# Local products of the first three sequences split between VectorE and GpSimd, late weights held back

## The reference

```python
x = x + local_attention(layernorm(x))            # each token sees itself and 3 tokens on each side
x = x + cross_attention(layernorm(x), ctx_1024)  # 120 context tokens
z = layernorm(x)                                 # then a block with its own residuals:
z = z + causal_attention(rmsnorm(z, n1_w))
z = z + silu(rmsnorm(z, n2_w) @ up.T) @ down.T * gate_factor
x = x + z
```

## Time and profile before

| | |
|---|---|
| median of 3 runs | 3523.06 us (3519.29 to 3523.43) |
| profiled execution: its time | 3525.48 us |
| its span | 3523.7 us |
| mean granted clock of TensorE | 0.986 |
| busy: TensorE / VectorE / ScalarE / GpSimd | 3421.1 / 2680.4 / 1829.9 / 2499.1 us |
| products of the local attention on GpSimd | 880.0 us (v) and 552.2 us (k) |
| their sums on VectorE | 294.4 us (v) and 291.7 us (k) |

### The profile page before, as it was taken

The page is one execution under the profiler, slowest core; times in us unless marked ns, Lnnn a source line. Parts: engine busy times, 40 slices in busy tenths (PEclk is TensorE's granted clock), DMA queues, the critical chain, the costliest instruction groups (busy, mean ns, idle before and its releaser), DMA issues.

```text
span 3523.7 us, 91852 instructions
## 1 busy us (share of the span) xinstructions
PE 3421.1 (97%) x36229; PEld 2775.1 (79%) x36229; DVE 2680.4 (76%) x5867; ACT 1829.9 (52%) x4241; POOL 2499.1 (71%) x3160
## 2 busy tenths in 40 slices
PE   5699999999999999999999999999999999999997
PEld 4477888888888888888888888888888888888876
DVE  5687787787787787787787787787787787787763
ACT  2345545545545545545545545545545545545542
POOL 5677777777777777777777777777777777777731
PEclk8799999999999999999999999999999999999998
DMA  5111221121121221121121221221121121121200
GB/s 169 61 52 47 69 77 47 69 77 47 69 77 47 69 77 47 69 77 47 69 77 47 69 77 46 69 77 47 69 77 47 69 77 47 69 77 47 69 8 10
DMA packets 90149, 223.31 MB, mean 63 GB/s; under 512 B 9286, under 2 KB 56706, under 8 KB 73346
## 3 DMA queue, kind: packets, MB, share of 16 engines
q1 hardware_dynamic: 89730, 217.44, 18.0%
HBM read 164.92 MB, written 50.39 MB: 61 GB/s over the span
## 4 chain that ended last, share of the span: by engine, by line
PE 95%; DVE 2%; ACT 1%; POOL 1%; DMA 0%; issue 0%; SPq 0%; DVEq 0%; ACTq 0%
PE ps L892 13%; PE ps L901 13%; PE ps L763 11%; PE ps L870 10%; PE ps L819 10%; PE ps L741 9%; PE ps L797 9%; PE ps L842 8%; PE ps L769 4%; PE ps L721 3%; PE ps L791 1%; PE ps L808 1%; PE ps L856 1%; ACT prob L1006 1%; DVE nmax L1328 1%; DMA y<-in_ctx 0%
## 5 line engine op out<-in xcount | busy, mean ns | idle before, releaser
L1162 POOL TENSOR_TENSOR chunks<-v_windows,xT 128x560 f32<-128x560 f32 (+1 forms) x384 | 880.0, 2302 | 85.5 <-DVE xT L1303 76.6
L1328 DVE TENSOR_REDUCE nmax<-ps 128x4 f32<-128x480 f32 (+2 forms) x1280 | 776.8, 671 | 178.0 <-PE ps L797 178.0
L1006 ACT ACTIVATE prob<-ps 128x256 f32<-128x256 f32 (+2 forms) x1536 | 670.5, 557 | 436.0 <-PE ps L819 436.0
L1157 POOL TENSOR_TENSOR chunks<-rest,k_windows 128x512 f32<-128x512 f32 (+1 forms) x384 | 552.2, 1454 | 366.7 <-DMA k_windows<-passed_on 291.7
L1282 DVE TENSOR_REDUCE held<-chunks 128x80 f32<-128x560 f32 (+1 forms) x384 | 294.4, 767 | 303.3 <-POOL chunks L1162 297.0
L892 PE MATMUL ps<-xT,w_up 128*128 128x256 f32 x2048 | 485.2, 385 | 1.6 <-ACT xT L959 1.6
L901 PE MATMUL ps<-w_down,held 128*128 128x256 f32 x2048 | 459.0, 382 | 1.9 <-DVE held L1381 1.6
L901 PEld LDWEIGHTS ps<-w_down,held 128*128 128x128 f32 x2048 | 383.9, 190 | 59.7 <-DVE held L1381 1.9
L892 PEld LDWEIGHTS ps<-xT,w_up 128*128 128x128 f32 x2048 | 375.2, 191 | 70.5 <-issue 20.2
L959 ACT COPY xT<-ps 128x512 f32<-128x512 f32 x256 | 153.1, 598 | 355.1 <-PE ps L721 355.1
L1174 POOL TENSOR_SCALAR_AFFINE_SELECT prob<-prob 128x512 f32<-128x512 f32 x512 | 310.9, 641 | 35.9 <-ACT prob L1006 35.8
(11 more groups left out here) (150 smaller groups left out, 6719.6 us busy)
## 6 DMA issues: line engine op xcount, KB each, us to landing
k_windows<-passed_on SPq DMA_DIRECT2D x64, 1024.0 KB, 5.0
v_windows<-passed_on SPq DMA_DIRECT2D x64, 1024.0 KB, 5.0
x<-in_x SPq DMA_DIRECT2D x64, 256.0 KB, 2.9
passed_on<-rest SPq DMA_DIRECT2D x64, 256.0 KB, 2.0
passed_on<-held SPq DMA_DIRECT2D x64, 256.0 KB, 3.4
out<-x SPq DMA_DIRECT2D x64, 256.0 KB, 2.2
y<-in_ctx SPq DMA_DIRECT2D x64, 120.0 KB, 2.8
held<-nmaxT SPq DMA_DIRECT2D x256, 8.0 KB
```

The costliest lines, as they stand in the source:

```text
L1006: last = nc.scalar.activation(prob_pair(seq, L, m)[0:keys, :, r, col:col + qs], of_pair, ACT.Exp, scale=SCALE)
L1157: last = nc.gpsimd.tensor_tensor(chunk_of(c).rearrange("p (j d) -> p j d", d=D), q_row, window("k", (b + first) * D, (D, n), (1, D)), ALU. ...
L1162: last = nc.gpsimd.tensor_tensor(chunk_of(c).rearrange("p (h i j) -> p h i j", i=HD, j=WINDOW), window("v", b * D + first * HD, (HD, n), ( ...
L1328: nc.vector.tensor_reduce(of_heads[:, ms[0]:ms[-1] + 1, :, r], src, AX_X, ALU.max, negate=True).then_inc(emptied[b], 1)
```

## The change

**What it does.** (a) For the first three sequences (EARLY = 3) the products of the even chunks 0, 2, 4, 6, 8, 10 move to VectorE; GpSimd keeps the odd ones. A helper, times, issues the same tensor_tensor on either engine. VectorE's products signal a new semaphore, doubled. The window buffers' next fetch waits for both engines, and GpSimd's chunks 1 and 7 wait for the windows and the softmax themselves, as chunks 0 and 6 did. From s3 on all twelve are GpSimd's. (b) BEHIND holds back two groups of weights in SyncE's list: group 3 is offered when the fetch of s0's k window has been issued, group 4 after that of its v window. (c) The constants that GpSimd writes at the start become a part of the plan, in the same place of its list. (d) Planner figures: transfers get a size and share an assumed wire, TensorE's parts take longer after an idle time, and busy times, lags and the cost of changing tiling are altered. These have no effect but on the lists.

Cut to the core; what is left out is the longer form of part(), further altered busy times of the same kind, and the constants' code, which moves as it is.

```diff
-Part = namedtuple("Part", "name args engine busy lag after takes gives")
-LAG = {"PE": 0.21, "ACT": 0.15, "DVE": 0.15, "POOL": 0.1}
+Part = namedtuple("Part", "name args engine busy lag after takes gives kb", defaults=(0,))
+LAG = {"SP": 1.1, "PE": 0.21, "ACT": 0.2, "DVE": 0.2, "POOL": 0.1}
 DMA_ISSUE = 0.42
 PLACES = {"lane": LANES, "prob": PROBS, "k_window": 1, "v_window": 1, "chunks": 1}
 
 DIVIDED = {"max": "rows", "scores": "rows", "values": "columns", "gate": "columns"}
-DIVIDE, REJOIN, CHANGE = 0.1, 0.2, 0.11
+DIVIDE, REJOIN, CHANGE = 0.1, 0.22, 0.15
+EASY_REJOIN = 0.13
+WIRE = 330.0
+LANDING = 1.1
+COOLS_AFTER, WARMS_IN = 1.5, 3.4
+EMPTIED = 0.24
+
+EARLY = 3
+EARLY_ON_DVE = {("window_times", (c,)): busy for c, busy in ((0, 0.92), (2, 0.65), (4, 0.65), (6, 0.8), (8, 0.7), (10, 0.7))}
+BEHIND = {("weights", (3,), "SP"): ("fetch", ("k",), "SP", 0), ("weights", (4,), "SP"): ("fetch", ("v",), "SP", 0)}
...
-    loads = [part("weights", (n,), "SP", busy, [], lag=lag)
-             for n, (busy, lag) in enumerate(((2.0, 5.0), (2.0, 6.0), (3.0, 10.0), (4.5, 12.0), (5.5, 18.0)))]
-    part("zeros", (), "SP", 0.6, [], lag=2.5)
+    loads = [part("weights", (n,), "SP", busy, [], lag=LANDING, kb=kb)
+             for n, (busy, kb) in enumerate(((1.9, 768), (1.9, 768), (2.8, 1280), (3.5, 1040), (4.0, 2060)))]
+    part("zeros", (), "SP", 1.2, [], lag=LANDING, kb=60)
+    constants = part("constants", (), "POOL", 5.1, [])
     banks = [("single", ("derive", (n,))) for n in range(2)]
-    tables = part("derive", ("tables",), "PE", 1.0, [], banks)
+    tables = part("derive", ("tables",), "PE", 1.0, [constants], banks)
     part("derive", ("tables",), "DVE", 1.4, [tables], (), banks)
-    part("derive", ("half",), "DVE", 0.9, [])
-    part("derive", ("bias",), "DVE", 4.6, [loads[3], ("derive", ("half",), "DVE")])
+    part("derive", ("half",), "DVE", 0.6, [constants])
+    part("derive", ("bias",), "DVE", 7.0, [loads[3], ("derive", ("half",), "DVE")])
...
+             ("turn", LOCAL): [("constants", (), "POOL")], ("turn_ctx", None): [("constants", (), "POOL")],
...
-                a = part(*step, "ACT", 2.0 if u < 2 else 2.3, [a] + first[1::2], (), [("quad", step)])
+                a = part(*step, "ACT", 1.95 if u < 2 else 2.15, [a] + first[1::2], (), [("quad", step)])
...
+           ("window_times", "DVE"): {"doubled": 1},
...
+        early = {i: EARLY_ON_DVE[p[:2]] for i, p in enumerate(parts) if p[:2] in EARLY_ON_DVE and p.engine == "POOL"}
+        released = {(who[3], at[who[:3]]): at[what] for what, who in BEHIND.items()}
+
+        def engine_of(n, i):
+            return "DVE" if n < EARLY and i in early else parts[i].engine
...
+            e = engine_of(n, i)
+            if e != "PE":
+                ready[e].append((n + due[i] + 0.001 * n, n, i))
+                ready[e].sort()
+
+        for i in released.values():
+            missing[0, i] += 1
         for n, i in todo:
-            if not parts[i].after:
+            if not missing[n, i]:
...
-                    end = now + p.busy
+                    busy = early[i] if e == "DVE" and i in early else p.busy
+                    end = now + busy
                     if e == "PE":
                         divides = DIVIDED.get(p.name)
                         if divides != divided:
-                            end += (CHANGE if divides and divided else
-                                    DIVIDE * bool(divides) + REJOIN * bool(divided))
+                            end += (CHANGE if divides and divided else DIVIDE if divides else
+                                    EASY_REJOIN if p.name == "shift" else REJOIN)
                         divided = divides
+                        if now - stopped > COOLS_AFTER:
+                            warmth = 0.0
+                        cold = min(2 * (end - now), WARMS_IN - warmth)
+                        warmth += cold
+                        end += cold / 2
+                        stopped = end
+                    landed = end
+                    if p.kb:
+                        wire = landed = max(wire, end) + p.kb / WIRE
                     for kind, use in p.gives:
                         if kind not in free:
                             banks = self.slot[kind, n, use]
                             for r, b in enumerate(banks):
-                                t = end - p.busy * (len(banks) - 1 - r) / len(banks) + p.lag
+                                t = end - busy * (len(banks) - 1 - r) / len(banks) + EMPTIED
                                 events.setdefault(round(t, 4), []).append(("empty", b, None))
                     events.setdefault(round(end, 4), []).append(("free", n, i))
-                    events.setdefault(round(end + p.lag, 4), []).append(("seen", n, i))
+                    events.setdefault(round(landed + (LAG[e] if e != p.engine else p.lag), 4), []).append(("seen", n, i))
...
-                    idle.add(parts[i].engine)
+                    idle.add(engine_of(n, i))
+                    j = released.get((n, i))
+                    if j is not None:
+                        missing[0, j] -= 1
+                        if not missing[0, j]:
+                            offer(0, j)
...
+        def times(engine, s, c):
+
+            w, b, first, n = CHUNKS[c]
+            if w == "k":
+                return engine.tensor_tensor(
+                    chunk_of(c).rearrange("p (j d) -> p j d", d=D),
+                    token_rows["q"][s][:, b, :].unsqueeze(1).to_broadcast([P, n, D]),
+                    window("k", (b + first) * D, (D, n), (1, D)), ALU.mult)
+            p = window_probs[s][:, b, :, first:first + n].rearrange("p j h -> p h j")
+            return engine.tensor_tensor(
+                chunk_of(c).rearrange("p (h i j) -> p h i j", i=HD, j=WINDOW),
+                window("v", b * D + first * HD, (HD, n), (1, HD), (D, WINDOW)),
+                p.unsqueeze(2).to_broadcast([P, n, HD, WINDOW]), ALU.mult)
...
+                            if before[0] < EARLY:
+                                sp.wait_ge(doubled[plan.lane[before[0]]],
+                                           reached["doubled", "window_times", before[0], (c - 1,)])
...
-                        if c == 0:
+                        if c == 0 or c == 1 and seq < EARLY:
                             wait_taken(pool, "project_rows", seq, "q")
 
                             pool.wait_ge(fetched["k"][s], reached["fetched", "fetch", seq, ("k",)])
-                        elif c == DOTS:
+                        elif c == DOTS or c == DOTS + 1 and seq < EARLY:
...
+                        times(nc.gpsimd, s, c).then_inc(multiplied[s], 1)
...
+                    elif name == "window_times":
+                        c, = args
+                        before = plan.before["chunks", seq, ()]
+                        if c >= 2:
+                            dve.wait_ge(reduced[s], reached["reduced", "window_reduce", seq, (c - 2,)])
+                        elif before:
+
+                            dve.wait_ge(reduced[plan.lane[before[0]]],
+                                        reached["reduced", "window_reduce", before[0], (len(CHUNKS) - 1,)])
+                        if c == 0:
+                            wait_taken(dve, "project_rows", seq, "q")
+
+                            dve.wait_ge(fetched["k"][s], reached["fetched", "fetch", seq, ("k",)])
+                        elif c == DOTS:
+
+                            dve.wait_ge(fetched["v"][s], reached["fetched", "fetch", seq, ("v",)])
+                            dve.wait_ge(weighted[s], reached["weighted", "window_sum", seq, ()])
+                        times(nc.vector, s, c).then_inc(doubled[s], 1)
                     elif name == "window_reduce":
                         c, = args
                         w, b, first, n = CHUNKS[c]
 
-                        dve.wait_ge(multiplied[s], reached["multiplied", "window_times", seq, (c,)])
+                        if seq < EARLY and ("window_times", (c,)) in EARLY_ON_DVE:
+                            dve.wait_ge(doubled[s], reached["doubled", "window_times", seq, (c,)])
+                        else:
+                            dve.wait_ge(multiplied[s], reached["multiplied", "window_times", seq, (c,)])
```

122 lines of the change are left out of this document (55 added, 67 removed).

## The result

The changed kernel takes 3543.6 us (median of 4 runs, 3542.6 to 3548.0); the kernel before, run beside it, takes 3523.2. The ratio is 1.0052, 95% interval 1.0040 to 1.0065: **slower by 0.5%**, where 3511 was forecast. The profiled execution took 3542.8, its span is 3541.1, 17.4 more than before.

What follows compares the result with a forecast made beforehand. TensorE, busy in 97% of the span, was taken as the bound. The start's gain of 18 us and the end's loss of 6 made -12: 3511 us against 3523.06, range 3496 to 3523.

Steps and rivals of the forecast that it cites:

- s4's transpose: TensorE's transpose of the fifth sequence's local result, at 241.23 before; forecast at 201, when its products end.
- the steady part: TensorE's order from just behind down(s1) to down(s60), claimed the same step for step; 52.89 us a sequence, no change.
- the end: Third scores of s63 now behind down(s62), so its values start 4.3 us later; 6 us lost in all, up to 10.
- Constants, planner figures and extra waits on signals already raised cost nothing I can see: A term of the sum, put at no cost.
- The passes: GpSimd's successive runs of twelve products for s0 to s4, forecast to end at 63, 90, 123 and, s3 and s4 together, 201.
- three modes: How both engines multiply: side by side saves 6.4 us per sequence; in turns, VectorE first 3.0 (taken), GpSimd first about 0.
- the rule that gave v 9.5 and 11.8: Pricing of a v pass with split products: 9.5 us side by side, 11.8 in turns with VectorE first; before, 14.2.
- the wait of s0: GpSimd's wait on VectorE in s0's pass: about 7 of 12.8 us go; 3 to 5 for late weights stay.
- What stands from down(s0) up to down(s1) is the same set of steps: TensorE's stretch from s4's transpose to down(s1), reckoned from its earlier 56.67 us: 55.3.
- the yardsticks: The forecast's yardstick was down(s1)'s start, after which all runs at TensorE's pace: 256.3, 18 us earlier than 274.38.
- The loads: Around s0's window fetch no late loads: 5.0 us in place of 7.4, and about 7 us of GpSimd's waits gone.
- rival 4: Slower: TensorE's fixed order waits for passes that are not early; 3539 us, decided by s4 ending after 220; chance 0.10.

Runs made afterwards that it cites:

- figs_behind: The changed kernel with no product on VectorE (EARLY = 0; new planner figures and held weights stay): 3543.9 us, ratio 1.0047 to the kernel before.
- behind_only: The kernel before with only the two late weight loads held behind the window fetches of s0 (old figures, no split): 3517.3 us, ratio 0.9971.
- split_behind: The changed kernel with the old planner figures throughout; the split and the held weights stay: 3516.3 us, ratio 0.9973 to the kernel before.

## Why the prediction was wrong

Against the profiled execution I had forecast -12, and the spans differ by +17.4. The 29 us between them, term by term: s4's transpose 9.2 (210.2 where 201 was forecast), from there to down(s1) 7.6 (62.9 for 55.3), down(s1) to down(s6) 2.9 (269.6 for the 266.6 of before), the steady part 4.7 (for nothing), the end 4.9 (10.9 for 6). The first alone would have left the result inside the range, at 3520; the other 20 us are what the new orders cost beyond what I gave them.

**"Constants, planner figures and extra waits on signals already raised cost nothing I can see": the step that failed**, a term put at nothing. The figures alone, with neither the split nor the held weights, cost 0.41% (figs_only). In the sum it stands in two places, the stretch to down(s1) and the steady part, both below.

**The passes: right in kind, short in size.** They end at 66.4, 95.5, 134.2 and 210.2 where 63, 90, 123 and 201 were forecast; between the last two stands 180.7 where 160 was forecast. Of the three modes I took VectorE first, in turns, and that is mostly what the rows show (two of the 18 products, at 32.23 and 49.63, start well within one of GpSimd's). GpSimd's and then VectorE's timeline of the changed kernel, s0 and s1 (in GpSimd's: v products of 560, 672 and 560, of which the first stands ahead of VectorE's product and the others behind it, and a k product of 512, alone 1.27):

```profile
49.28 2.15 POOL L630 TENSOR_TENSOR chunks<-v_windows,xT 128x560 f32<-128x560 f32 x1 [5.77 <-DVE xT L1368]
57.74 3.33 POOL L630 TENSOR_TENSOR chunks<-v_windows,xT 128x672 f32<-128x672 f32 x1 [6.30 <-DVE held L1347]
62.63 2.91 POOL L630 TENSOR_TENSOR chunks<-v_windows,xT 128x560 f32<-128x560 f32 x1 [1.56 <-DVE held L1347]
66.39 2.04 POOL L625 TENSOR_TENSOR chunks<-rest,k_windows 128x512 f32<-128x512 f32 x1 [0.85 <-DVE held L1347]
```

```profile
29.77 0.96 DVE L625 TENSOR_TENSOR chunks<-rest,k_windows 128x768 f32<-128x768 f32 x1 [3.01 <-DMA k_windows<-passed_on]
...
49.63 3.02 DVE L630 TENSOR_TENSOR chunks<-v_windows,xT 128x672 f32<-128x672 f32 x1
...
57.58 1.11 DVE L630 TENSOR_TENSOR chunks<-v_windows,xT 128x560 f32<-128x560 f32 x1
...
66.35 0.96 DVE L625 TENSOR_TENSOR chunks<-rest,k_windows 128x768 f32<-128x768 f32 x1
...
80.18 1.34 DVE L630 TENSOR_TENSOR chunks<-v_windows,xT 128x672 f32<-128x672 f32 x1
```

Whoever starts second is the longer by most of what is left of the other's product: at 49.63 VectorE by 1.68 of 1.80 (3.02 against 1.34 at 80.18), at 57.74 and 66.39 GpSimd by 0.78 of 0.95 and 0.77 of 0.92. The Trainium skill (SBUF — State Buffer, Who interferes with whom) says that a VectorE instruction with two SBUF inputs and a GpSimd instruction that reads SBUF block each other, whichever starts second; these rows agree. VectorE's k products cost what I gave them (0.95, 0.68), its v products 1.12 and 1.34 where I had 0.73 and 0.85: I priced all by the element, from a sum over a k chunk and an addition. V's products read across windows, which k's don't; that this makes them dearer fits, but no run separates it. Two terms of the working were off as well. By the rule that gave v 9.5 and 11.8, k comes to 7.1 and 9.4, not 7.7 and 8.8, so the saving in turns is 2.4 a sequence and not 3.0, and with the measured v products some 1.1 (an estimate from these rows). And the wait of s0 was short. The 6.30 us that GpSimd waits at 57.74 lie behind the scaling of the late weights on VectorE, which was busy without a gap from 43.49 to 64.57. Together the passes were 9 late, within the bounds that I had set (192 to 212). But most of the 31 us is not the split's: the new figures alone bring s4's transpose to 219.26, 22 of them, and in the changed kernel the largest gain of a pass, from one transpose to the next, is in s4's, whose products are GpSimd's alone. I had s3 and s4 together 9.4 shorter; in fact s3's pass became 4.6 longer and s4's 14.8 shorter.

**"What stands from down(s0) up to down(s1) is the same set of steps", so 55.3: where it failed in the start.** The set is the same, the time is 62.9. I took the stretch at its time in the old order, less its one wait of 0.92. In the new order TensorE comes to its steps before what they need is there: the rows above show 1.94 us for a softmax, 2.26 for scores whose shifted maxima were issued by SyncE at 265.47, in all 5.7 us of gaps, and matmuls below full clock behind them (granted 0.74 from 253.70 to 256.20: 2.50 for cross values that take 1.94 in the kernel before; down(s1) 8.25 for 7.17). The 31 us of earlier transposes then buy almost nothing. The runs show it as the figures' doing: down(s6) comes 0.9 to 6.7 us later than before in all eight kernels with new figures, whole or in part, in the start, and 6.8 to 8.4 earlier in the three with old figures and held weights there. Down(s0) to down(s1) takes 56.7 to 56.8 in the kernels with the old start, 59.1 and 59.5 with the new figures and no split, 62.4 in the changed kernel; so about half of what this stretch lost comes only with the split, though by down(s6) no loss of the split is left. And the yardsticks themselves were poor: from figs_behind to the changed kernel, the split moves s4's transpose 12 us earlier and down(s1) not at all (272.63, 273.18), and in figs_only down(s1) is 4.3 earlier than before and down(s6) 4.2 later, so TensorE does not run at its steady pace from down(s1) on.

**The loads: about right, but not in this kernel.** I counted 2.4 us of landing and about 7 of waits, inside the passes. Alone the held weights gave 8.5 us at the first transpose and 9 to 10 in time (medians and ratio), evenly to the end, more than I had put down for that run; it is the only part of the change that gains, and under the new figures nothing of it shows.

**The steady part, "the order of the change is the same": true of TensorE's order only.** I compared that engine's alone. VectorE's differs in every sequence, and costs some 1 to 5 us.

**The end: right mechanism, undersized.** The wait before the values was named and its place was right; 4.3 forecast, 5.14 measured, and the lower clock behind it, which I had as a possibility up to 10 in all, came: 10.9.

**The rivals.** The time that rival 4 gave, 3539, was nearest, but not by its mechanism: it decides if s4's transpose comes after 220, and it came at 210. None of my cases had both fast passes and a late down(s1). That is why the range missed: I had spread it over prices of the products, and taken an order made anew as free.

**Versions.** The fastest kernels of this study are behind_only (0.9971) and split_behind (0.9973), which differ by nothing that can be measured: the held weights under the old figures beat both the kernel before and the changed one.

## What to carry over

When a planner's figures change, every engine's order is a change of its own: compare all of them, the steady part included, and put the new figures in alone before crediting what came with them. A milestone that moves early is worth only what the bound engine can use; look at its idle time in the stretch behind it. What paid here was the simplest part, large late loads held behind the transfer that the first work waits for.

## What I had not expected of the hardware

One 2.2 us product of GpSimd ahead of its moments instead of behind them, in each steady sequence, gave 52 waits of TensorE, 22.3 us, with two steps of VectorE moved as well, TensorE's order untouched and TensorE still 99% busy there (495 of 500 us). And a gap of TensorE that the profile puts down to "issue" need not be one: ahead of these scores the kernel waits for SyncE's two 8 KB transfers of shifted maxima, whose landing the trace doesn't record. From their issue at 265.47 to the scores at 270.26 it is 4.8 us, of which 1.1 is issue; in the steady part, from 1356.39 to 1360.91, it is 4.5.

```profile
265.47 1.10 SPq L723 DMA_DIRECT2D held<-nmaxT  x2
```
